# Expert layer: the gather of the token tile three ahead is issued in odd steps, ahead of the accumulating store, and the loads of gate weights wait for both parts of the one before

## The reference

```python
logits = x @ gate_w.T + gate_b                       # 32 experts
topk_logits, topk_idx = top_k(logits, 4)
topk_weight = softmax(topk_logits)
gate = ragged_dot(xt, w_gate, group_sizes) + b_gate[gid]    # 1024 -> 512
up   = ragged_dot(xt, w_up, group_sizes) + b_up[gid]
gate, up = minimum(gate, 7), clip(up, -7, 7)
outs = ragged_dot((up + 1) * gate * sigmoid(1.702 * gate), w_down, group_sizes) + b_down[gid]
y = sum(outs * topk_weight, over the 4 experts of a token)
```

## Time and profile before

| | |
|---|---|
| median of three runs | 3703.39 us (3698.12 to 3704.42) |
| profiled execution | 3702.42 us |
| its span, first to last instruction | 3700.7 us |
| mean granted TensorE clock | 0.985 |
| TensorE matmuls busy | 3543.4 us, 96% |
| VectorE, ScalarE, GpSimd busy | 51%, 22%, 21% |
| HBM read and written | 523.13 and 41.40 MB, 153 GB/s over the span |
| gathers (L1668), stores (L1681) | 37 and 69 |

### The profile page before, as it was taken

One profiled execution on the slowest core, in us unless ns is written; L12 is line 12 of the kernel. 1 busy time (PEld: TensorE's weight loads), 2 busy tenths in 40 slices (PEclk: granted clock), 3 DMA queues, 4 the chain that ended last, 5 costly groups with the idle time before them and its releaser, 6 DMA issues.

```text
span 3700.7 us, 38052 instructions
## 1 busy us (share of the span) xinstructions
PE 3543.4 (96%) x14156; PEld 1749.4 (47%) x14157; DVE 1871.3 (51%) x1726; ACT 827.4 (22%) x1358; POOL 790.5 (21%) x745
## 2 busy tenths in 40 slices
PE   7899999999999969999999989999999999999999
PEld 4455455445445433333333345545455454554554
DVE  7785476468348451111111147638457286562561
ACT  1221032022022211111111125234143152220110
POOL 5600400320130012222222221000000011581660
PEclk9999999999999989999999989999999999999999
DMA  5621221122113176988888964335244151330320
GB/s 186 234 93 50 74 87 68 57 71 92 51 35 137 50 276 231 330 318 318 293 316 290 367 221 167 130 113 184 87 154 167 51 180 54 119 136 18 136 102 36
DMA packets 95088, 562.50 MB, mean 152 GB/s; under 512 B 11304, under 2 KB 13480, under 8 KB 77056
## 3 DMA queue, kind: packets, MB, share of 16 engines
q1 hardware_dynamic: 60784, 450.79, 31.9%
q0 software_dynamic: 30880, 93.75, 9.3%
q10 hardware_dynamic: 3312, 16.37, 1.3%
HBM read 523.13 MB, written 41.40 MB: 153 GB/s over the span
## 4 chain that ended last, share of the span: by engine, by line
PE 81%; DMA 7%; DVE 6%; issue 2%; ACT 2%; POOL 1%; SPq 1%; POOLq 0%; DVEq 0%; ACTq 0%
PE PS L856 12%; PE PS L842 12%; PE PS L1732 10%; PE PS L2050 9%; PE PS L992 9%; DMA bias<-in_b 5%; PE PS L1756 5%; PE PS L2064 4%; PE PS L724 4%; PE PS L741 3%; PE PS L979 2%; PE PS L819 2%; PE PS L753 1%; PE PS L862 1%; DVE sums L1249 1%
## 5 line engine op out<-in xcount | busy, mean ns | idle before, releaser
L856 PE MATMUL PS<-Sb,kvN 128*128 128x400 f32 (+1 forms) x1536 | 540.2, 501 | 2.8 <-ACT Sb L1095 2.8
L842 PE MATMUL PS<-qc,kvT 128*128 128x400 f32 x1536 | 529.4, 501 | 11.8 <-ACT Sb L1104 3.9
L1732 PE MATMUL PS<-W,hT 128*64 128x512 f32 x2208 | 507.0, 602 | 16.9 <-DMA bias<-in_b 14.7
L842 PEld LDWEIGHTS PS<-qc,kvT 128*128 128x128 f32 x1536 | 290.6, 190 | 239.7 <-ACT Sb L1104 7.7
L1310 POOL TENSOR_TENSOR qrope<-rt,rt 128x400 f32<-128x400 f32 x192 | 208.8, 1108 | 790.0 <-DVE rt L1200 789.9
L856 PEld LDWEIGHTS PS<-Sb,kvN 128*128 128x128 f32 (+1 forms) x1536 | 283.5, 191 | 198.0 <-ACT Sb L1095 4.8
L1825 DVE TENSOR_TENSOR gu<-PS,bias 128x512 f32<-128x512 f32 x69 | 47.7, 691 | 639.3 <-PE PS L1732 639.3
L2050 PE MATMUL PS<-xh,wq 128*128 128x400 f16 x2048 | 348.8, 334 | 0.9 <-DVE xh L1164 0.9
L992 PE MATMUL PS<-wb,ctxl 128*128 128x512 f32 x768 | 331.7, 593 | 4.2 <-ACT ctxl L1019 4.2
L2006 POOL TENSOR_SCALAR gtq<-stg,thr 128x1024 f16<-128x1024 f32 x96 | 289.6, 3033 | 200.2 <-DMA stg<-in_F 133.0
L1233 DVE TENSOR_REDUCE mx<-Sb 128x400 f32<-128x2400 f32 x64 | 270.9, 4232 | 102.4 <-ACT Sb L1104 102.4
(11 more groups left out here) (281 smaller groups left out, 3466.0 us busy)
## 6 DMA issues: line engine op xcount, KB each, us to landing
W<-in_W SPq DMA_DIRECT2D x96, 2048.0 KB, 12.1
kvT<-kvT_d SPq DMA_DIRECT2D x64, 768.0 KB, 5.7
kvN<-kvN_d SPq DMA_DIRECT2D x64, 768.0 KB, 4.3
stg<-in_F SPq DMA_DIRECT2D x32, 1536.0 KB, 6.4
absin<-in_F POOLq DMA_DIRECT2D x48, 512.0 KB, 3.7
hn<-in_F POOLq DMA_DIRECT2D x48, 512.0 KB, 3.8
wb<-in_WB SPq DMA_DIRECT2D x8, 2560.0 KB, 9.0
wc_h<-in_WC SPq DMA_DIRECT2D x32, 576.0 KB, 4.5
```

The lines of the kernel that those rows point to most:

```text
L842: mm = nc.tensor.matmul(PS[:, lc % 3, 0:GW], kvT[b % 2][:, dc, lc * P:(lc + 1) * P], qc[:, dc, b, :], start=dc == 0, stop=dc == CC - 1)
L856: mm = nc.tensor.matmul(PS[:, value_bank(b) + dc, 0:GW], kvN[b % 3][0:k, lc, dc * P:(dc + 1) * P], Sb[b % 3][0:k, lc, :], start=lc == 0, s ...
L1732: mm = nc.tensor.matmul(PS[g * BS:(g + 1) * BS, 2 + u % 2, :], hT2[k][:, c, half * BS:(half + 1) * BS], W2[:, q, o:o + N1], start=c == 0, ...
```

## The change

GpSimd: in odd step s = 2t + 1, behind the gate column and ahead of the store of step s - 1, the gather of tile t + 3 is issued; even steps issue none, except that step 0 issues the gather of tile 2 first. SyncE: ahead of each load in the loop one semaphore increment and one wait more, for the first part (`m_wga`) of the load before. VectorE works out the last step directly and the count of gathers from the number of steps; the table of indices has one column more.

```diff
-        idx = pm.put("idx", [P, MAX_TILES + 2], I32)
+        idx = pm.put("idx", [P, MAX_TILES + 3], I32)
...
-            link(dve, ts(np_i[0:1, 0:1], rounds[0:1, :], float(NQ_W), -1.0, ALU.mult, ALU.add))
-            vt.tensor_copy(np_i[0:1, 2:3], np_i[0:1, 0:1])
+            ts(np_i[0:1, 2:3], rounds[0:1, :], float(NQ_W), -1.0, ALU.mult, ALU.add)
+            link(dve, ts(np_i[0:1, 0:1], rounds[0:1, :], float(NQ_W), None, ALU.mult))
             link(dve, ts(np_i[0:1, 0:1], np_i[0:1, 0:1], 1, None, ALU.arith_shift_right))
...
                 sp.wait_ge(sem("m_wg"), GU_INC * (i - 1))
+                sp.sem_inc(sem("go"), 1)
+                sp.wait_ge(sem("m_wga"), DN_INC * (i - 1))
                 sp.wait_ge(sem("m_gu"), done)
...
             def one(it, u):
                 s, head = it * IT + u, isinstance(it, int) and it == 0
-                if u % G == 0:
-                    gather(it * (IT // G) + u // G + 2, (u // G) % 2)
                 if head and u == 0:
+                    gather(2, 0)
                     pool.wait_ge(sem("m_gs"), 2 * G)
                     pool.wait_ge(sem("m_fill"), 16 * HG)
                 gate_column(s, u % 2)
+                if u % G == 1:
+                    gather(it * (IT // G) + u // G + 3, (u // G + 1) % 2)
                 if not (head and u == 0):
                     scatter(s - 1, (u - 1) % 2, (u - 1) % 2, not (head and u == 1))
...
-            gathered = [pool.value_load(np_i[0:1, 3 + k:4 + k], min_val=16, max_val=8 * (MAX_TILES + 3)) for k in range(2)]
+            gathered = [pool.value_load(np_i[0:1, 3 + k:4 + k], min_val=16, max_val=8 * (MAX_TILES + 4)) for k in range(2)]
```

## The result

The changed kernel takes 3712.97 us (median of 19 runs, 3703.21 to 3724.56); the kernel before, run beside it, 3705.34 us (19 runs, 3697.66 to 3714.46). The ratio is 1.0016, with an interval of 1.0009 to 1.0023: slower by about 6 us (the two medians are 7.6 apart), which by the ratio is still within 0.2%. The profiled execution took 3714.27 us with a span of 3712.5. Lines of the expert layer carry numbers higher by 2 to 3 than before: the gather is L1670, the store L1683, the matmuls L1732 and L1724 are L1735 and L1727, ScalarE's L1891 is L1894.

What follows compares the result with a forecast made beforehand. TensorE, busy 96% of the span, was taken as the bound, with expert-layer waits on bias rows and weights. Only gather bytes counted: 3702.42 + 1.8 = 3704.2 us, 3705.2 on the median's level; range 3697 to 3713.

Steps and rivals of the forecast that it cites:

- The gather as slack: Expert layer: TensorE never waited for a gathered tile, tightest slack 3.2 us, so issuing gathers earlier gains 0.
- Bytes in front of weights: Expert layer: three moved gathers land partly ahead of awaited weights, costing 0.2, 0.9 and 0.7 us, sum 1.8.
- dense stretch: Expert-layer time with all 16 DMA engines full: 1340 to 1440, 1600 to 1682, and one ending near 1797 us.
- clock tips: TensorE waits growing past a length between 2.13 and 3.02 us slow the matmuls behind; two would add 3.3 us.
- Turns between queues: DMA engines alternating queues packet by packet would push gathers through at weights' expense: 4.1 us in place of 1.8.
- SyncE's wait: One increment and wait more ahead of each weight load: 0 taken, at most 2.5 us over 11 loads.
- GpSimd's new issues: GpSimd's wait for a transpose, index copy, semaphore and gather issue ahead of the store fit under TensorE's matmuls: 0.
- A: Rival: weight loads absorb the 1.8 us, waits stay at 14.7; 3703.4 us or a little less, chance 0.21.
- B: Rival: waits at 1416.90, 1435.98 and 1645.23 shorten and clock cost goes; 9.8 us faster, 3693.6, chance 0.08.
- C: Rival: gathers ahead of stores delay each second store, ScalarE waits for its buffer; some 51 us slower, 3754, chance 0.03.
- D: Rival: bytes and clock bounds together, 10.7 us slower, 3714; chance 0.08 including what lies between 7.4 and 11.
- E: Rival: the moved gathers push all their bytes ahead of the weights; 4.1 us slower, 3707.5, chance 0.08.

Runs made afterwards that it cites:

- kernel 4: The kernel before, with the gather issued one store later instead of one store earlier; 3758.98 us, ratio 1.0141.
- kernel 6: The changed kernel with its gather held back until the previous store has landed and ScalarE's next output is there; 3726.95 us, ratio 1.0054.
- kernel 2: The kernel before with only SyncE's added semaphore increment and wait ahead of each load, gathers unmoved; 3705.46 us, ratio 0.9991.

## Why the prediction was right, and where it was not

The time, 3712.97 us, is inside the range, at its slow edge, and the change is within 0.2%: +6 us by the ratio where +1.8 was forecast. That it is inside is in part luck: the edge is 3713, and more than half of the slowdown comes from a place that the sum did not have.

**The gather as slack, 0: right.** No wait on a gathered tile before or after, and kernel 4 shows what lay on the other side of the 3.2 us found in the earlier trace rows.

**Bytes in front of weights, 1.8 us: near the size found, but not stretch by stretch.** Over the five full-size profiles of either order (4 and 6, whose gather is elsewhere, left out) the layer's mean is 818.5 and 821.2, so 2.7 us, with ranges of 816.2 to 819.7 and 819.5 to 824.5. The profile after is the extreme one. Timed in the same ten profiles from the layer's start to VectorE's bias addition (L1825 before) behind each dense stretch, the changed order costs -0.6 us in the first, 1.3 in the second and 1.4 in the third, 2.1 together, where 0.2, 0.9 and 0.7 stood. Behind the third, and against the profile before, the order of before lies at -3.1 to 0.0 us and the changed one at 0.0 to +3.5. What is left to 2.7 is mostly the wait near 2128 of one profile. The timings agree: the ratios of the five kernels average 1.0016, 5.8 us, and less 3.6 to 3.9 for the rest that leaves some 2.

The forecast issues at 1433.4, near 1672 and near 1788.1 came at 1435.7, 1673.5 and 1790.2. The waits near 1682 and 1797 came out at 2.33 and 2.93 where "near 2" and "near 3" stood. Three things were not in the sum: the matmuls behind the wait of 2.33 took 5.18 us in place of 3.65, so one of the two clock tips that I had kept for the bounds did happen, and not where the list of signs had it; those behind the shorter wait near 1437 took 3.65 in place of 5.97, which gave 2.3 back; and the wait near 2128, outside the three stretches I looked at. The premise that a wait longer than some length between 2.13 and 3.02 tips the clock is not borne out: 2.33 did, 2.86 and 2.93 did not.

That the cost goes with the bytes is not shown. With half of them the orders are 1.4 us apart at the layer's end, but 2.6 behind the third dense stretch, on one profile each. TensorE's waits on bias and weights alone don't separate the orders: 13.7 to 17.1 us before, 15.0 to 21.1 after.

**Turns between queues.** The changed flights that lie wholly in dense stretches take as long as the 16.1 us of the earlier trace rows: the gathers of 1383.4, 1619.9 and 1763.5 landed after 15.4, 15.4 and 15.6 us. Two of the three moved ones can be read, those of 1435.67 and 1673.48, with 8.7 and 10.7, but their stretches ended before they landed. So the choice of shares by the flight stands, as far as flights tell, and what was measured, 2.1 us, is nearer to its 1.8 than to 4.1; the scatter does not decide. Taking turns packet by packet (the Trainium skill, "DMA: Bandwidth & Descriptors", section "Queues, rings and completion order") is what stood behind the 4.1, and no run here shows how the turns go.

**SyncE's wait, 0: right**, kernel 2 is 0.9991 (0.9981 to 1.0000) of the kernel before. **GpSimd's new issues, 0: right** for the layer: 23.5 us of waiting for transposes, behind which nobody is late; ScalarE waits 19.4 us for stores, where "near 23.5" stood.

**The rest of the kernel, tacitly 0: wrong.** The step that failed is the sentence "The change touches only the expert layer". GpSimd's program also runs the loads of line 1320 some 550 us behind the layer, and 3.6 to 3.9 us, more than half of the slowdown, arose there. The last of the signs named ahead of the result ("if the span outside 1331 to 2165 changes by more than 2 us") is the one that turned up.

**The rivals.** A (nothing felt) is unlikely for the layer, by the 2.1 us behind the third stretch where the two orders only touch; at the layer's end their ranges overlap by 0.2 us. B (faster) falls: the waits near 1436 and 1645 did get shorter (2.58 and 3.32 us for 4.04 and 4.3), but that near 1417 grew to 3.73, the one at 1430 from 1.87 to 2.86, and all waits on bias and weights together went from 16.6 to 21.1 us. C (gather delays store) did not happen in the changed kernel, but kernel 6 shows that the mechanism is real when the gather goes out right in front of the store (layer 844.2 against 818.5 us, 1.0054 in all, gathers that came late included). D's 10.7 us were not reached, though one of its clock tips was; E cannot be told from the forecast.

## What to carry to other kernels

A transfer that nobody waits for gains nothing from an earlier start, and it can put its bytes ahead of something that is waited for; try it once in the other direction, as kernel 4 did, to learn how much slack there was to buy. When a queue carries two kinds of transfer, the lead of one over the other decides: 8 to 11 us in front did it no harm, held back to right in front cost 23 us in all (3726.95 against 3704.21). And split the span of every pair of profiles by stage before explaining a few microseconds, since an edit to an engine's program can shift that engine by tenths of a microsecond in a stage that it does not name, and change by how much one transfer goes ahead of another. Take several profiles of either kernel too: the wait near 2128, which made most of the layer's difference in the first pair, was in none of the repeats.

## What was not expected of the hardware

GpSimd has a pause of some 0.44 us ahead of one load in the third head group (1.08 to 1.09 us behind its release where nearly all other loads have 0.64 to 0.67), at a place that depends on the kernel. Where the 0.79 MB of another queue start 0.06 or 0.07 us behind instead of 0.50, the first tile arrives 2 us later, and the kernel loses almost 4. The profiles show these together; no run changed the 0.44 us alone. The granted clock is not set by the length of one wait: x16 matmuls behind waits of 2.58, 2.86 and 2.93 us took 3.65 us, behind a wait of 2.33 they took 5.18.
